# Where the stores of the halves stand, which chunks carry the splitting, and in what order a layer takes its kept chunks

## The chip, the cores and the metric

The kernel runs on one core of one Trainium2 chip. The metric is the device time of one execution in microseconds (us). The core has TensorE (PE, matmul), VectorE (DVE), ScalarE (ACT), GpSimd (POOL) and SyncE (SP, which here only issues transfers), all of which run their own instruction streams and meet at semaphores.

## What is computed

A graph network over 3125 nodes with 64 features and 103125 edges, four blocks one after another, each adding its result to x. Three places matter here:

```python
h = max(layernorm(x), 0)
# block 0: ten hops with the unweighted adjacency (counts)
h0 = h @ W + b
for _ in range(10):
    agg = segment_sum((h * norm_src)[src], dst)
    h = 0.9 * agg * norm_dst + 0.1 * h0
x = x + h
# block 1: three layers with the weighted adjacency (float32 edge weights)
h = max(layernorm(x), 0)
for W, b in (1, 2, 3):
    h = segment_sum((h @ W)[src] * norm[:, None], dst) + b     # ReLU after the first two
x = x + h
# block 2: attention over the edges; before it
h = layernorm(max(layernorm(x), 0)) * g + b ;  q, k, v = h @ Wq, h @ Wk, h @ Wv
```

## The kernel before

Both adjacency matrices are held densely. The unweighted one (`counts`, float16) stays in SBUF. The weighted one was written to HBM by `stage_build` as 196 blocks of 16 destination nodes (`aw`, float32, 128 x 400 each, 200 KB). Nodes are 25 rows of 128 (`NCH`); destinations are computed in 7 chunks (`NDC`): six of 512 columns and a seventh, narrow one of 64.

**Hops, `stage_layer0_hops` (L770).** Ten hops of seven chunks. PE, for each chunk c: the product (25 matmuls of 128x512, L840) into bank c % 4, then `back(t, c - 1)` (L824), eight small matmuls that turn the chunk before it, for which ACT must have copied that chunk from its bank (`copied`, L874). DVE then mixes it into the next hop's operand (`mix`, L961 to L965). The count of mixed chunks, `mixed`, gates the next hop's product.

Beside it the float32 blocks are split for the layers into a high and a low float16 half. For each block i: SP loads it into `ring[i % 4]` (L906), DVE sums its columns (`reduce`, L926, counted by `reduced`), ACT casts the high half (`high`, L867), POOL subtracts to get the low half (L895, `lo_done`). Two blocks fill one of two buffers `split`, and SP stores the pair (400 KB, L908, `halves`). ACT's first cast into a buffer waits for that buffer's store (`stored`); a load into the ring waits for `reduced` and `lo_done` of the block that was there. Each pair of hops handles 40 blocks (the last one 36), four behind each chunk until they are used up: all seven chunks of the even hop, and three of the odd one. ACT's order is: copy of chunk c, its four casts, copy of chunk c + 1. DVE's order is: mix of chunk c, its four reduces. After every eight blocks PE turns a column of sums into degrees (`degrees`, L833).

SP's loop, per four blocks, before:

```python
for k in range(4):
    sp.wait_ge(reduced, g * 4 + (k - 3)); sp.wait_ge(lo_done, g * 4 + (k - 3))
    sp.dma_start(ring[k], ...)              # load of block 4g + k
    if k % 2:
        sp.dma_start(halves[...], flat(k // 2))     # store of a pair of four blocks ago
```

**Layers, `stage_layer1` (L984).** Three layers of seven chunks. A chunk of the weighted matrix is read back as 16 stored pairs (L1018). Chunks 0 to 4 (`STREAM` = 5) are streamed in each layer through two buffers of `m.big`; chunk 5 and the narrow chunk 6 are loaded once and kept. PE's product is 50 matmuls of 128x512 (L1047) and up to four for the self loops (L1052); `back` (L1064) multiplies the chunk before by W. A load into a streamed buffer waits on SP until the product that read it is done (`prod_done`). After a layer DVE takes a maximum, POOL spreads it (L1093), and DVE halves the new operand (`halve`, L1106 and L1107), for which the next layer's first product waits. Order of chunks: 0 to 6. The three W and b (nine transfers) are issued by SP after the first two big loads; PE waits for them (`s_in`) after the first product. ACT's first work in the stage is a sqrt for the norm.

**Attend tables, `stage_attend_tables` (L1211).** Ten small loads, PE transposes Wk, Wv and We once all ten have landed (L1263), DVE copies them (L1324 to L1327) and the product with Wp (L1330), and then runs two norms over 128x1600 (L568 to L576, with L1333 between), two products (L1336, L1337), and `hn` goes to HBM and to PE. POOL clears a region in the beginning (L1258).

## Time and profile before

| what | us |
|---|---|
| median of 3 runs | 4331.68 |
| lowest, highest | 4321.05, 4349.07 |
| the profiled execution, its own time | 4306.86 |
| its span | 4305.1 |
| mean granted TensorE clock | 0.817 of full speed |
| hops, from PE's first product to the next stage | 870.3 to 1366.4 |
| layers | 1366.4 to about 1694 |
| attend tables | about 1695 to 1754 |

The profile is one execution, with start and duration of each instruction and, for each engine's idle time, the instruction or transfer that ended it. Busy times of engines overlap. A granted clock of 1.00 is 2.4 GHz, 0.50 is 1.2 GHz; a mean between them is a stretch with both. SPq rows are SP issuing a transfer, not the transfer itself. Median landing times run from the issue to the data's arrival.

### The profile page before, as it was taken

How to read it: one execution, taken by the hardware profiler on the slowest of the kernel's cores; microseconds unless marked ns; L12 is line 12 of the kernel's file. 1: busy time of each engine (PE TensorE's matmuls, PEld its weight loads, DVE VectorE, ACT ScalarE, POOL GpSimd, SP SyncE). 2: the span in 40 equal slices, each digit the busy share in tenths (PEclk: the TensorE clock that was granted, in tenths of full speed). 3: DMA queues.
4: the chain of work that ended last, by engine and by line, in shares of the span. 5: the costliest groups of instructions: out<-in, count | busy, mean ns of one | idle time of the engine just before them, and what ended most of it. 6: DMA issues, size and time to landing. Idle time of an engine off the chain costs nothing. (4 is left out here: it accounts for less than half of the span.)

```text
span 4305.1 us, 80877 instructions
## 1 busy us (share of the span) xinstructions
PE 3180.1 (74%) x17608; PEld 2011.1 (47%) x17608; DVE 1986.0 (46%) x6727; ACT 1584.7 (37%) x4586; POOL 1621.8 (38%) x1763
## 2 busy tenths in 40 slices
PE   3787877778886686477777777777764777787777
PEld 2444444444443343356656656656652444444445
DVE  5666666555555112344444444444743444444442
ACT  1555555222221000233333333333422444444444
POOL 2000000033332000466666666665005666666660
PEclk6899898989997888687787887777956888888885
DMA  1111111155556974322222222222102222222220
GB/s 32 58 59 58 59 58 60 34 161 153 158 176 228 377 305 185 72 54 54 53 55 55 55 54 53 55 54 54 31 2 60 62 65 65 66 63 65 66 59 9
DMA packets 417246, 370.53 MB, mean 86 GB/s; under 512 B 175145, under 2 KB 341769, under 8 KB 416873
## 3 DMA queue, kind: packets, MB, share of 16 engines
q1 hardware_dynamic: 367512, 316.11, 23.1%
q0 software_dynamic: 46144, 48.98, 6.2%
q8 instruction: 192, 3.15, 0.3%
q14 instruction: 182, 1.48, 0.1%
q10 hardware_dynamic: 3216, 0.82, 0.1%
HBM read 279.70 MB, written 86.00 MB: 85 GB/s over the span
## 5 line engine op out<-in xcount | busy, mean ns | idle before, releaser
L1413 POOL DMA_INDIRECT big<-row_table,src x806 | 762.9, 947 | 542.7 <-issue 185.0
L1731 POOL DMA_INDIRECT big<-message_table,src x610 | 611.3, 1002 | 331.7 <-DVE big L1858 174.1
L1438 PE MATMUL banks<-big 97*128 x902 | 400.3, 534 | 142.2 <-issue 136.3
L1454 PE MATMUL banks<-big 128*128 x1804 | 348.8, 326 | 174.0 <-ACT big L1470 109.8
L486 PE MATMUL banks<-work 128*128 128x226 f16 x1197 | 350.3, 293 | 147.0 <-issue 131.4
L1454 PEld LDWEIGHTS banks<-big 128*128 128x128 f32 x1804 | 313.9, 245 | 200.8 <-issue 200.3
L1769 PE MATMUL banks<-big 128*128 128x512 f16 x1225 | 393.6, 439 | 14.1 <-DVE big L1846 14.1
L840 PE MATMUL banks<-big,work 128*128 128x512 f16 (+1 forms) x1750 | 354.7, 362 | 17.8 <-DVE work L973 17.4
L1503 DVE TENSOR_REDUCE big<-banks 128x1 f32<-128x256 f32 x451 | 189.8, 421 | 334.6 <-PE banks L1438 190.2
L1470 ACT COPY big<-banks 128x256 f32<-128x256 f32 x451 | 170.1, 377 | 453.6 <-remote 201.8
L1778 PE MATMUL banks<-big 128*64 x1804 | 246.7, 267 | 122.2 <-issue 106.8
L1778 PEld LDWEIGHTS banks<-big 128*64 128x64 f32 x1804 | 173.1, 163 | 348.8 <-issue 348.1
L487 PE MATMUL banks<-work 128*128 128x200 f16 x1197 | 335.7, 280 | 0.0
L488 PE MATMUL banks<-work 128*128 128x200 f16 x1197 | 327.1, 273 | 0.0
L895 POOL TENSOR_TENSOR work<-work 128x400 f16<-128x400 f32 x196 | 184.0, 961 | 322.0 <-ACT work L867 322.0
L486 PEld LDWEIGHTS banks<-work 128*128 128x128 f16 x1197 | 121.9, 102 | 373.8 <-issue 360.5
L1520 DVE SCALAR_TENSOR_TENSOR big<-big,banks 128x97 f32 x451 | 142.7, 316 | 325.9 <-remote 193.3
L429 POOL COPY work<-work 128x100 f16<-128x100 f16 x120 | 35.9, 300 | 666.9 <-DVE work L452 649.8
L512 ACT ACTIVATE work<-banks 128x800 f32<-128x800 f32 x196 | 164.5, 839 | 330.0 <-PE banks L488 330.0
L1864 DVE TENSOR_SCALAR big<-big 128x512 f16<-128x512 f16 x1225 | 282.2, 286 | 3.2 <-issue 0.2
L1047 PE MATMUL banks<-big,work 128*128 128x512 f16 x900 | 218.1, 407 | 86.4 <-DMA big<-weights_halves 49.9
L1858 DVE TENSOR_TENSOR big<-banks,big 128x128 f32<-128x128 f32 x305 | 87.4, 287 | 411.9 <-remote 290.0
(320 smaller groups left out, 5863.6 us busy)
## 6 DMA issues: line engine op xcount, KB each, us to landing
big<-weights_halves SPq DMA_DIRECT2D x16, 6400.0 KB, 20.3
weights_dense<-work SPq DMA_DIRECT2D x196, 200.0 KB, 1.9
work<-weights_dense SPq DMA_DIRECT2D x196, 200.0 KB, 3.1
weights_halves<-work SPq DMA_DIRECT2D x98, 400.0 KB, 3.7
big<-q_table SPq DMA_DIRECT2D x451, 64.0 KB
big<-in_ef SPq DMA_DIRECT2D x403, 64.0 KB
big<-in_ea SPq DMA_DIRECT2D x403, 32.0 KB
big<-row_table,src POOLq DMA_INDIRECT x806
```

Of the source, the lines that this page charges most:

```text
L486: pe.matmul(to(CW, CW + CAW), rows[:, 0, t, :], cols[:, t, :], start=False, stop=True, skip_group_check=True)
L487: pe.matmul(to(0, CW), rows[:, 1, t, :], cols[:, t, 0:CW], start=False, stop=True, skip_group_check=True)
L488: pe.matmul(to(0, CW), rows[:, 2, t, :], cols[:, t, 0:CW], start=False, stop=True, skip_group_check=True).then_inc(vis_done, 1)
L840: ins = pe.matmul(m.PB[c % 4][:, 0:width(c)], z[k][:, a, :, :], counts[:, a, c * DC:c * DC + width(c)], start=(a == 0), stop=(a == NCH - 1))
L1047: pe.matmul(out, z[l % 2][:, a, :, :], st[buffer(l, c)][:, 0:n // BP, s, a * BP:(a + 1) * BP], start=(a == 0 and s == 0), stop=False)
L1413: po.indirect_dma_start(rows[:, t % RT, s, 0:D], None, x_t.rearrange("a p c -> (a p) c"), bass.IndirectOffsetOnAxis(ap=m.src2[:, s, t:t + ...
L1438: pe.matmul(psS[v % 2], qT[v % R][0:XW, :], XF[0:XW, bass.ds(slot, 1), :].rearrange("p t e -> p (t e)"), start=False, stop=True).then_inc( ...
L1454: ins = pe.matmul(psA[v % 2], PT[v % 2][:, s * P:(s + 1) * P], rows[:, bass.ds(slot, 1), s, :].rearrange("p t c -> p (t c)"), start=(s == ...
L1731: po.indirect_dma_start(G[n % R][:, s, :], None, g_t.rearrange("a p c -> (a p) c"), bass.IndirectOffsetOnAxis(ap=m.src2[:, s, t:t + 1], ax ...
L1769: pe.matmul(psH[q % 2], table[:, a, :, :].rearrange("p s d -> p (s d)"), hot[n % HOT], start=(a == 0), stop=(a == NCH - 1)).then_inc(hot_u ...
L1778: ins = pe.matmul(psA[v % 4], oh[v % 4][:, s, :], M[:, bass.ds(slot, 1), s, :].rearrange("p t c -> p (t c)"), start=(s == 0), stop=(s == 1))
L1864: dve.tensor_scalar(hot[n % HOT], key[q % 2], float(P * a - CENTER), None, ALU.is_equal).then_inc(hot_ready, 1)
```

## The change

It has five parts.

1. In the hops SP stores a pair as soon as both its blocks are split, ahead of the two loads into their ring places, and without waiting for their `reduced`.
2. Blocks are dealt out as four behind each of chunks 0 to 4 of every hop (`SUMMING` = 5), none behind chunks 5 and 6. `degrees` moves to the steps 4, 6, 9, 11, 13 of a pair's fourteen.
3. In the layers the chunks are taken in the order 0, 1, 5, 2, 3, 6, 4: the kept ones stand between the streamed ones. Chunk 5 is loaded before the narrow one. Counters go by the place in that order.
4. The nine small weights are issued by ACT, ahead of its sqrt.
5. In the attend tables DVE runs the first norm before it waits for the transposes, and the second one before it copies the product with Wp.

```diff
+def blocks_after(k, c, n):
+    at = 4 * (SUMMING * k + c)
+    return range(at, min(n, at + 4)) if c < SUMMING else range(0)
+SUMMING = 5
+DEGREES_AT = (4, 6, 9, 11, 13)
...
-                    if at in (4, 6, 8, 10, 12):
-                        degrees(pair, (at - 4) // 2, isinstance(pair, int) and pair == 0)
+                    if at in DEGREES_AT:
+                        degrees(pair, DEGREES_AT.index(at), isinstance(pair, int) and pair == 0)
...
-                    for i in range(4 * (NDC * k + c), min(summed_in(pair), 4 * (NDC * k + c) + 4)):
+                    for i in blocks_after(k, c, summed_in(pair)):
                         high(pair, i)
...
-                for k in range(4):
-                    sp.wait_ge(reduced, g * 4 + (k - 3))
-                    sp.wait_ge(lo_done, g * 4 + (k - 3))
-                    sp.dma_start(ring[k], aw[bass.ds(g * 4 + k, 1), :, :].rearrange("j p c -> p (j c)")).then_inc(w_landed[k], 16)
-                    if k % 2:
-                        sp.dma_start(halves[bass.ds(g * 2 + (k // 2 - 2), 1), :, :].rearrange("j p c -> p (j c)"),
-                                     flat(k // 2)).then_inc(stored[k // 2], 16)
+                for i in range(2):
+                    sp.wait_ge(lo_done, g * 4 + (2 * i - 2))
+                    sp.dma_start(halves[bass.ds(g * 2 + (i - 2), 1), :, :].rearrange("j p c -> p (j c)"), flat(i)).then_inc(stored[i], 16)
+                    for k in range(2 * i, 2 * i + 2):
+                        sp.wait_ge(reduced, g * 4 + (k - 3))
+                        sp.dma_start(ring[k], aw[bass.ds(g * 4 + k, 1), :, :].rearrange("j p c -> p (j c)")).then_inc(w_landed[k], 16)
...
+        ORDER = (0, 1, STREAM, 2, 3, NDC - 1, 4)
...
             load(0, 0)
             load(0, 1)
-            for i in range(3):
-                for half in range(2):
-                    sp.dma_start(w_sb[i][half * D:(half + 1) * D, :], wts[i]).then_inc(s_in, 16)
-                sp.dma_start(b_sb[i], biases[i].partition_broadcast(P)).then_inc(s_in, 16)
+            load(0, STREAM)
             load(0, NDC - 1)
-            load(0, STREAM)
             for n in range(2, 3 * STREAM):
                 l, c = divmod(n - 2, STREAM)
-                sp.wait_ge(prod_done, l * NDC + c + 1)
+                sp.wait_ge(prod_done, l * NDC + ORDER.index(c) + 1)
                 load(n // STREAM, n % STREAM)
...
-                u = l * NDC + c
+                u = l * NDC + ORDER.index(c)
...
-                for c in range(NDC):
+                for i, c in enumerate(ORDER):
                     product(l, c)
...
-                    if c:
-                        back(l, c - 1)
-                back(l, NDC - 1)
+                    if i:
+                        back(l, ORDER[i - 1])
+                back(l, ORDER[-1])
...
         def _(act):
+            for i in range(3):
+                for half in range(2):
+                    act.dma_start(w_sb[i][half * D:(half + 1) * D, :], wts[i]).then_inc(s_in, 16)
+                act.dma_start(b_sb[i], biases[i].partition_broadcast(P)).then_inc(s_in, 16)
...
+            dve_norm(dve, chain, h, xs, tmp, (mean, var), s_var, s_std, 1)
+            chain(dve.tensor_scalar(h, h, 0.0, None, ALU.max))
             dve.wait_ge(s_wt, 1)
             dve.tensor_copy(u_k[:, 0:D], m.PB[6][:, 0:D])
...
+            dve_norm(dve, chain, hn, h, tmp, (mean, var), s_var, s_std, 2)
+            dve.wait_ge(s_in, 160)
             dve.wait_ge(s_wo, HEADS)
...
-            dve_norm(dve, chain, h, xs, tmp, (mean, var), s_var, s_std, 1)
-            chain(dve.tensor_scalar(h, h, 0.0, None, ALU.max))
-            dve_norm(dve, chain, hn, h, tmp, (mean, var), s_var, s_std, 2)
-            dve.wait_ge(s_in, 160)
```

## Rows read from the trace of the kernel before

**Rows 1.** Stretches (start:end, length; busy and count of engines; PE clock, DMA share, GB/s).

```profile
870.26:1366.37 496.11, 419.24 (x2300) 225.28 (x2300) 282.07 (x537) 125.05 (x266) 184.00 (x196) 0.92 0.54 164
1366.37:1693.02 326.65, 242.70 (x1275) 118.86 (x1275) 61.42 (x145) 11.65 (x23) 1.09 (x3) 0.86 0.81 325
1497.00:1516.00 19.00, 15.89 (x66) 6.88 (x67) 6.50 (x23) 0.59 (x1) 0.35 (x1) 0.82 0.19 62
1377.00:1399.00 22.00, 13.29 (x54) 5.63 (x54) 10.79 (x26) 0.81 (x2) 0.38 (x1) 0.73 1.03 417
```

**Rows 2.** The same view: hops 4, 5 and 9, from first product to next.

```profile
1068.49:1122.27 53.78, 41.16 (x230) 22.53 (x230) 32.68 (x63) 14.45 (x31) 21.41 (x24) 0.91 0.51 152
1122.27:1165.96 43.69, 41.74 (x233) 22.13 (x232) 25.63 (x51) 10.85 (x23) 16.03 (x18) 0.95 0.63 188
1315.35:1363.95 48.60, 45.40 (x232) 23.88 (x231) 18.77 (x35) 9.15 (x19) 12.19 (x14) 0.87 0.44 136
```

**Rows 3.** Waits in the hops: engine, line, for what, total us, times, longest.

```profile
ACT work L867 <- DMA weights_halves<-work: 268.6, 87, 8.3
```

**Rows 4.** Order of time, end of hop 4: start, duration, engine, line, [idle before].

```profile
1110.65 0.95 ACT L867 CAST work<-work 128x400 f16<-128x400 f32 x2 [2.65 <-DMA weights_halves<-work]
1111.26 1.84 POOL L895 TENSOR_TENSOR work<-work 128x400 f16<-128x400 f32 x2 [2.24 <-ACT work L867]
1113.87 0.36 SPq L908 DMA_DIRECT2D weights_halves<-work  x1
...
1115.48 1.97 PE L824 MATMUL banks<-work 128*128 128x64 f32 x8 [5.59 <-ACT work L874]
1117.71 0.95 ACT L867 CAST work<-work 128x400 f16<-128x400 f32 x2 [2.29 <-DMA weights_halves<-work]
1122.27 12.91 PE L840 MATMUL banks<-big,work 128*128 128x512 f16 x50
```

**Rows 5.** Order of time, beginning of hop 4.

```profile
1079.30 1.00 PE L824 MATMUL banks<-work 128*128 128x64 f32 x8
1083.24 1.07 SPq L906 DMA_DIRECT2D work<-weights_dense  x2
1085.53 1.00 PE L824 MATMUL banks<-work 128*128 128x64 f32 x8
```

**Rows 6.** Order of time, layers 0 and 1, PE.

```profile
1404.43 13.48 PE L1047 MATMUL banks<-big,work 128*128 128x512 f16 x50 [6.38 <-DMA work<-in_L_gnn_b]
...
1500.11 13.41 PE L1047 MATMUL banks<-big,work 128*128 128x512 f16 x50 [4.65 <-DVE work L1107]
...
1513.58 10.96 PE L1047 MATMUL banks<-big,work 128*128 128x512 f16 x50
...
1533.27 13.91 PE L1047 MATMUL banks<-big,work 128*128 128x512 f16 x50 [7.61 <-DMA big<-weights_halves]
```

**Rows 7.** The page's DMA issues: out<-in, count, size of each, median us to landing.

```profile
big<-weights_halves SPq DMA_DIRECT2D x16, 6400.0 KB, 20.3
work<-weights_dense SPq DMA_DIRECT2D x196, 200.0 KB, 3.1
weights_halves<-work SPq DMA_DIRECT2D x98, 400.0 KB, 3.7
```

**Rows 8.** DVE's line L963 in the hops: duration in ns, min/median/max.

```profile
L963 DVE CAST work<-work x63: 186/293/999, 884.7 to 1317.0; 128x256 f16<-128x256 f32 x54, 64x64 f16<-64x64 f32 x9
```

**Rows 9.** Order of time, hop 9.

```profile
1332.34 0.42 DVE L956 TENSOR_TENSOR work<-banks,colsN 128x256 f32<-128x256 f32 x1 [9.86 <-DMA work<-in_x]
1344.85 1.97 PE L824 MATMUL banks<-work 128*128 128x64 f32 x8 [3.20 <-ACT work L874]
```

**Rows 10.** Order of time, attend tables.

```profile
1695.18 5.43 POOL L1258 MEMSET big<- 32x6400 f32 x1 [96.79 <-POOLq L987]
1705.38 1.81 DVE L568 TENSOR_REDUCE colsN<-work 128x25 f32<-128x1600 f32 x1
1730.75 0.38 SPq L1247 DMA_DIRECT2D row_table<-work  x1
```

More of the change, by code:

```diff
@@ L965, in mix @@
                         dve.tensor_scalar(zn[0:rows, a, 1, :], tc, LO, None, ALU.mult).then_inc(mixed, 1)
-                    for i in range(4 * (NDC * k + c), 4 * (NDC * k + c) + 4):
-                        if i < summed_in(pair):
-                            reduce(pair, i)
+                    for i in blocks_after(k, c, summed_in(pair)):
+                        reduce(pair, i)
                 if k:
@@ L1043, in product @@
                 for a in range(NCH):
-                    if c == 0 and a % GROUP == 0:
+                    if c == ORDER[0] and a % GROUP == 0:
                         pe.wait_ge(s_z, l * NG + a // GROUP + 1)
@@ L1056, in back @@
             def back(l, c):
-                u = l * NDC + c
+                u = l * NDC + ORDER.index(c)
                 pe.wait_ge(copied, u + 1)
@@ L1067, in _ @@
             for l in range(3):
-                for c in range(NDC):
+                for i, c in enumerate(ORDER):
                     product(l, c)
-                    if l == 0 and c == 0:
+                    if l == 0 and i == 0:
                         pe.wait_ge(s_in, 144)
-                    if c:
-                        back(l, c - 1)
-                back(l, NDC - 1)
+                    if i:
+                        back(l, ORDER[i - 1])
+                back(l, ORDER[-1])
         @block.scalar
         def _(act):
+            for i in range(3):
+                for half in range(2):
+                    act.dma_start(w_sb[i][half * D:(half + 1) * D, :], wts[i]).then_inc(s_in, 16)
+                act.dma_start(b_sb[i], biases[i].partition_broadcast(P)).then_inc(s_in, 16)
             for n in range(2):
@@ L1085, in _ @@
                     act.wait_ge(back_done, u - 1)
-                n = width(u % NDC)
+                n = width(ORDER[u % NDC])
                 nc.scalar.copy(rt[u % 2][:, 0:n], m.PB[u % 3][:, 0:n]).then_inc(copied, 1)
@@ L1127, in _ @@
             for u in range(3 * NDC):
-                l, c = divmod(u, NDC)
+                l, c = u // NDC, ORDER[u % NDC]
                 dve.wait_ge(back_done, u + 1)
@@ L1144, in _ @@
                     dve.tensor_tensor(xs[0:rows, a, :], xs[0:rows, a, :], tc, ALU.add).then_inc(mixed, 1)
-                if l < 2 and c == NDC - 1:
+                if l < 2 and c == ORDER[-1]:
                     dve.wait_ge(mixed, u + 1)
```

## The prediction

> **What bounds the kernel now.** I read the table by stretch first, because the diff touches three adjacent stages only. The hops take 496.1 us with PE busy for 419.2; the three layers take 326.7 us with PE busy for 242.7 while DMA averages 325 GB/s, although it runs at 417 when it is fed and drops to 62 in the 19 us around a layer's turn [rows 1]. So the hops wait on something short and frequent, and the layers stream from HBM with holes in the stream.
>
> Hops: an even hop costs 53.8 us and an odd one 43.7, with equal PE work [rows 2]. ACT spends 268.6 us waiting for stores of halves [rows 3], mostly harmless. The order of time shows where it is not: ACT casts a pair at 1110.65, POOL splits it until 1113.10, the store leaves at 1113.87, and the next cast into that buffer is at 1117.71: 7.06 us for a loop that returns once a chunk, against a PE cadence of 1085.53 - 1079.30 = 6.23 us [rows 4, 5]. ACT therefore falls behind. Its copies, queued behind four casts, come late, most of all at the narrow seventh chunk, where PE waits 5.59 us; then the eight matmuls take 1.97 us, not 1.00, and the next two products 12.91, not 10.96 [rows 4, 5, 6]. In an odd hop chunks 3 to 6 have no casts, so its tail is free.
>
> **Hops, a floor.** The odd hop lasts 43.69 with PE idle for 1.95 [rows 2]; 1.95 more is the cold clock (12.91 - 10.96). About 0.5 of the idle time belongs to the turn of the hops. Without waits a hop is 43.7 - 1.95 - 1.4 = 40.3 us.
>
> **Hops, after.** Each hop has 20 blocks in chunks 0 to 4, none in 5 and 6. SP issues a pair's store as soon as it is split, then the two loads. I walk one hop with back(0) at 0 (1079.30). The first load of chunk 1's blocks still waits for `reduced`: 3.94 [rows 5]. Landing takes 3.1, of a store 3.7 [rows 7]. So chunk 1's first cast is at 7.05, the four casts end at 10.1 (the second store waits behind two loads: issue 5.2, landed 8.8), and copy(2) ends at 10.7; PE needs it at 12.46, so it is in time. The loop now is cast to split done 2.45, store issue 0.25 instead of 0.77 (no loads ahead), landing 3.84: 6.5 us. Chunks 2, 3 and 4 start their casts at 13.5, 20.0, 26.5; copies 3 and 4 end at 17.2 and 23.7, due at 18.7 and 25.1. But copy(5) ends at 26.5 + 3.1 + 0.6 = 30.2, and PE, past a narrow product of 0.7, wants it at 26.7: a wait of 3.5. The tail wait survives, and now every hop has one.
>
> DVE's mix is at risk: a cast there took between 293 and 999 ns [rows 8], the long ones while POOL split. In my walk POOL splits from 7.65 to 11.45 and mix(1) begins at 7.3, so it may be pushed by up to 2.3 us, its reduces and the loads behind them too. Walked again with that, copy(3) is 0.5 late, copy(4) 0.1, copy(5) 4.8: 5.4 of waits. I take 4.4, between the two. A wait of 3.20 was followed by matmuls at half pace [rows 9], so I add the clock: 0.9 on the late matmuls, 2.0 on the next products. A hop: 40.3 + 4.4 + 2.9 = 47.6. Before, the first nine take 1315.35 - 870.26 = 445.1, or 49.45 each; gain 1.85 x 9 = 16.6 (ends: 25 and 8.5).
>
> The Trainium skill's "SBUF — State Buffer" (SBUF: two separate sides) says that a VectorE op in a 2-port mode, or with two SBUF inputs against a GpSimd op that reads SBUF, waits out the whole GpSimd op; the 999 ns agree. By it alone the first nine hops would gain the 8.5.
>
> Last hop: 36 - 20 = 16 blocks end in chunk 3, so no tail wait. Before, 48.6 with DVE waiting 9.86 for x [rows 2, 9], since ACT issued that load between casts; now no cast stands after the last chunks of hop 8, it leaves before back(0) of hop 9 by some 13 us and is hidden. After: 40.3 + 2.0 = 42.3, gain 6.3. The last store leaves at 26.7 and lands at 30.4 by the walk, when DVE ends its last mix: I charge 1 for the end of the stage. Hops together: 16.6 + 6.3 - 1 = 22 (14 to 30).
>
> **Layers.** The bytes stay: 16 loads of 6,400 KB, at 417 GB/s 15.7 us each [rows 1, 7]. What changes is when the two streaming buffers come free. Before, c = 5 and 6 are computed last, so for some 24 us PE frees nothing, and after both prefetches have landed DMA stands still until the next layer's first product is done. Then the third chunk is late: product 1 of layer 1 starts at 1513.58, when product 0 ended, and product 2 at 1533.27, so 19.7 us from free to landed [rows 6].
>
> Walk after, t = 0 at the first load. Landings: chunk 0 17.7, 1 33.4, kept 5 49.1, kept 6 51.1, then 2, 3, 4 at 67.1, 82.8, 99 without a hole, and layer 1's chunk 0 at 114.5. PE is bound by them in layer 0 and ends its chunk 4 at 110.5. A turn stays at 5.9 (copy, back, mix, max, halve; a full chunk is last, but only one mix follows), so product (1,0) runs from 116.4 to 129.7. Landed: (1,1) 130.2, (1,2) 129.7 + 19.5 = 149.2, (1,3) 164.9. PE computes (1,1) until 141.6, kept 5 until 153.5, (1,2) until 165.4, (1,3) until 177.3, 6, then (1,4), landed 184.9, until 197.5. Layer 2 likewise: (2,0) 203.4 to 216.7, (2,1) to 228.6, kept 5 to 240.4, (2,2) to 252.3, (2,3) to 264.2, (2,4) landed 271.9, done 284.5, back 286.4. Each warm product is 10.96 + 0.9 for own and back; cold ones 12 to 13.4 [rows 6]. Before: 326.65. Gain 40 (34 to 46: the 19.5 stands four times in the chain, each perhaps 1 off, and a cold product more or less is 1 to 2).
>
> In layer 0 the small weights stand in SP's queue behind two big loads, and product (0,1) waited 6.38 for the last bias, until 1404.43, t = 38.1 [rows 6], where its chunk was there at 33.4. On ACT's queue they leave at once; the 4.6 us are in the walk. Nine issues at the 0.36 of SP's store [rows 4], or a little more, take ACT 3 to 5 us; its first sqrt is due some 8 us in (three quarters of one of the two norms that share the tables' 25.3 us, below). The Trainium skill's "DMA: Bandwidth & Descriptors" (Issuing engines are not separate DMA queues) says that all queues share the 16 engines and only issue time is saved; that is how it is costed.
>
> **Attend tables.** DVE's chain starts at 1705.38 only because PE's transposes waited for ten loads; it ends at 1730.72, and the stage starts at 1695.2 [rows 10]. Norms first: 1695.2 + 25.3 + 1.0 for the six copies now between = 1721.5, gain 9.2. Against it: POOL's memset lasts until 1700.6 [rows 10] and the norm's second instruction may stand behind it for 3.5: gain 5.7. I take 7. The same page on SBUF names that lock for a 2-port VectorE op; by it the gain is 5.7. No run shown has the two together.
>
> **Sum.** 22 + 40 + 7 = 69 us. The profiled execution took 4306.86 (span 4305.1), 25 below the median of 4331.68, 14 below the fastest run. On the median: 4331.7 - 69 = 4263 (1.6%).
>
> **Rivals.**
> 1. The tail wait shrinks so far that the clock does not fall. With landings 0.6 shorter the first cast is at 6.4 and the loops keep PE's pace of 6.3, so copy(5) ends at 25.3 + 3.7 = 29.0 and PE waits 2.3, about the odd hop's 1.95 of short waits, whose granted clock stayed at 0.95 [rows 2]. A hop is then 40.3 + 2.3 = 42.6: gain 6.85 x 9 + 6.3 - 1 = 67, and 4331.7 - 114 = 4218 in all. For: less is in flight at a time, since the first store leaves early. Against: the collisions with POOL lengthen the loop. Chance 0.14.
> 2. The hops gain nothing: full collisions in every chunk, and only the last hop profits (5), layers 36, tables 5: 4331.7 - 46 = 4286. Chance 0.17.
> 3. Layers gain only 15: small issues on ACT stand behind the big loads as on SP's queue, and the sqrt, DVE's norm and the first product start up to 16 late; or freed buffers refill later. 4331.7 - 22 - 15 - 7 = 4288. Against: ACT's queue is not the one that the big loads fill, and it landed x in mid-traffic within 10 us [rows 9]. Chance 0.07.
> 4. Slower: loads are now queued behind a store of 400 KB that waits for both blocks' split, so the blocks' arrival, not the store, closes the loop. If it closes in 9.0 us, waits are 3.5 + 4 x 2.5 = 13.5 and the clock costs 2.9 + 4 x 1.0, a hop 60.7; nine lose 101 and the total is 4331.7 + 101 - 52 = 4381. It decides from 7.65 us: 3.5 + 2.9 + 4 x 2.15 = 15.0 makes a hop of 55.3, 5.8 x 9 = 52, which is all that the last hop, layers and tables give. Against: by the walk a load leaves 0.9 after the split and lands at 4.0, beside the store's 4.1. Chance 0.04.
>
> **Chances.** My forecast 0.58. Range 4210 to 4300: rivals 1 to 3 in it. The measurement tells about 1% (43 us) from no change. Faster by over 1%: all of the forecast but a corner, rival 1, most of 2, half of 3: 0.84. Within 1%: 0.12. Slower: 0.04.
>
> **What would show it.** Even and odd hops of equal length, 46 to 49 us, with one PE wait for ACT of 3 to 5 us at the seventh chunk and almost none in mid-hop; the store's issue 0.25 after POOL's end; a last hop near 42. Layers of about 286 us, DMA over 370 GB/s, no hole at the turns over 5 us, PE's waits for loads only before (1,4), (2,4) and in layer 0. DVE's reduce of the norm beginning at once after the layers. I am wrong if tail waits vanish, if mid-hop waits for `w_landed` appear, or if ACT's first sqrt is late.

## The result

| kernel | median us | lowest to highest |
|---|---|---|
| before, 4 runs | 4339.62 | 4321.05 to 4349.07 |
| changed, 4 runs | 4271.28 | 4263.59 to 4278.55 |

The ratio is 0.9847, 95% interval 0.9805 to 0.9890: 68 us or 1.5% faster, where 69 us was forecast. The profiled executions alone, 4306.86 and 4278.55, differ by only 28: attention and the nodes stage behind it, which the diff leaves as they were, took 1480 us together in the one and 1511 in the other, and the messages stage another 10 more. Stage by stage, up to where the attention begins, the trace is the better measure. The hops are counted from PE's first product, the layers from SP's first load, tables and attention from DVE's or POOL's first instruction, all to about 0.1 us.

| stage | before | changed | gain | forecast |
|---|---|---|---|---|
| hops | 496.1 | 466.7 | 29.4 | 22 |
| layers | 328.8 | 292.9 | 35.9 | 40 |
| attend tables | 59.6 | 58.3 | 1.3 | 7 |
| attention begins at | 1754.8 | 1685.8 | 69.0 | |

The three gains make 66.7; the hops also began 2.2 earlier in this execution, with which the diff has nothing to do. So the sum is right and its terms are each off. First the changed kernel's stretches (columns as in [rows 1]): hops, layers, 19 us around the first turn of the layers, hops 5 and 4, the last hop.

```profile
868.02:1334.69 466.67, 424.02 (x2300) 232.02 (x2300) 305.85 (x537) 130.60 (x266) 186.71 (x196) 0.91 0.53 174
1334.69:1625.83 291.14, 239.06 (x1275) 117.72 (x1275) 62.10 (x147) 11.64 (x23) 1.09 (x3) 0.89 0.92 364
1449.00:1468.00 19.00, 14.61 (x64) 6.70 (x63) 8.23 (x26) 0.59 (x1) 0.35 (x1) 0.82 1.02 402
1104.99:1152.42 47.43, 43.28 (x232) 23.69 (x231) 31.69 (x56) 13.25 (x27) 18.86 (x20) 0.90 0.52 170
1057.60:1104.99 47.39, 42.68 (x230) 23.38 (x230) 31.89 (x57) 13.25 (x27) 19.12 (x20) 0.90 0.53 173
1291.91:1332.43 40.52, 40.51 (x232) 22.12 (x231) 23.20 (x41) 11.43 (x23) 15.25 (x16) 0.97 0.55 182
```

Against [rows 1, 2]: even and odd hops are equal, at 47.4. In the last one PE waits for nothing. DMA moves 364 GB/s through the layers where it moved 325 (the forecast's sign was over 370), and 402 at the turn where it moved 62: the hole is closed. ACT's wait in the hops is no longer for the stores ([rows 3]), for which it now never waits, but for the ring's loads:

```profile
ACT work L877 <- DMA work<-weights_dense: 198.7, 112, 5.7
```

The walk through a hop, in order of time in hop 5 (back(0) is at 1118.39, so 0 of the forecast's walk):

```profile
1118.39 1.00 PE L834 MATMUL banks<-work 128*128 128x64 f32 x8
1122.33 1.07 SPq L918 DMA_DIRECT2D work<-weights_dense  x2
1124.81 0.53 ACT L877 CAST work<-work 128x400 f16<-128x400 f32 x1 [5.63 <-DMA work<-weights_dense]
...
1131.84 0.53 ACT L877 CAST work<-work 128x400 f16<-128x400 f32 x1 [2.37 <-DMA work<-weights_dense]
...
1132.44 2.03 POOL L905 TENSOR_TENSOR work<-work 128x400 f16<-128x400 f32 x2 [2.08 <-ACT work L877]
1132.55 1.12 DVE L971 TENSOR_TENSOR work<-work 128x256 f32<-128x256 f32 x1
...
1133.70 0.92 DVE L972 CAST work<-work 128x256 f16<-128x256 f32 x1
...
1138.84 0.53 ACT L877 CAST work<-work 128x400 f16<-128x400 f32 x1 [2.48 <-DMA work<-weights_dense]
...
1145.12 0.53 ACT L877 CAST work<-work 128x400 f16<-128x400 f32 x1 [1.61 <-DMA work<-weights_dense]
...
1149.80 1.97 PE L834 MATMUL banks<-work 128*128 128x64 f32 x8 [4.00 <-ACT work L884]
...
1152.42 12.05 PE L850 MATMUL banks<-big,work 128*128 128x512 f16 x50
```

The load leaves at 3.94, as before [rows 5]. The first casts of chunks 1 to 4 are at 6.4, 13.5, 20.5 and 26.7 (walk: 7.05, 13.5, 20.0, 26.5), and PE waits 4.00 at the narrow chunk (4.4). Between two of these casts stand 7.0, 7.0 and 6.3 us, and each of them waits for a load. Over hops 0 to 8 PE's wait at the narrow chunk is 3.7 to 4.8, and PE waits in mid-hop only three times, 0.8 at most.

### The profile page after: what moved, and what is told of

It is laid out like the page before. It is cut to its first block and busy times, and to the rows that moved or that the text cites. A ratio compares the mean times of both kernels' runs of the same rounds, so it can differ in the third digit from the quotient of the medians.

```text
span 4276.8 us, 80686 instructions
## 1 busy us (share of the span) xinstructions
PE 3229.8 (76%) x17608; PEld 2043.7 (48%) x17608; DVE 2012.0 (47%) x6727; ACT 1587.1 (37%) x4586; POOL 1616.9 (38%) x1763
## 5 line engine op out<-in xcount | busy, mean ns | idle before, releaser
L1447 PE MATMUL banks<-big 97*128 x902 | 408.9, 545 | 149.0 <-issue 125.8
L1447 PEld LDWEIGHTS banks<-big 97*128 97x128 f32 x902 | 180.4, 248 | 200.3 <-issue 198.4
L1821 ACT ACTIVATE big<-iotaH,rel 128x64 f32<-128x64 f16 x902 | 259.1, 335 | 17.0 <-DVE big L1839 15.5
```

The costliest lines, as they stand in the source:

```text
L1447: pe.matmul(psS[v % 2], qT[v % R][0:XW, :], XF[0:XW, bass.ds(slot, 1), :].rearrange("p t e -> p (t e)"), start=False, stop=True).then_inc( ...
L1821: ins = nc.scalar.activation(away[v % 2][:, s, :], m.iotaH[:, 0:BD], ACT.Abs, bias=m.rel2[:, s, v:v + 1], scale=-1.0)
```

## The experiments

All twelve runs were made on other chips than the first, where the kernel before takes 3903 to 3910 us instead of 4340. The stages ahead of the attention take the same time on all of them: the changed kernel's attention begins at 1685.8 and 1686.6, and a stage that an experiment leaves as it was agrees with the first chip's within some 5 us. So stages are compared, each from one profile. What the same code gives in the changed kernel is the measure of noise: hops 463.5 to 469.0, layers 291.3 to 293.5, tables 53.6 to 58.3. The difference between the chips lies behind these stages; see the last section.

| run | hops | hops 0 to 8, mean | layers | tables | attention begins at |
|---|---|---|---|---|---|
| before | 496.1 | 49.45 | 328.8 | 59.6 | 1754.8 |
| changed | 466.7 | 47.10 | 292.9 | 58.3 | 1685.8 |
| changed again (e12) | 466.3 | 46.89 | 293.5 | 58.3 | 1686.6 |
| store order only (e1) | 456.6 | 45.92 | 330.8 | 59.6 | 1715.0 |
| dealing only (e2) | 500.8 | 50.35 | 327.7 | 59.6 | 1757.3 |
| layers only (e3) | 493.9 | 49.72 | 294.0 | 64.2 | 1719.9 |
| weights on SP (e4) | 466.0 | 46.94 | 294.2 | 56.4 | 1685.5 |
| tables as before (e5) | 463.5 | 46.72 | 293.1 | 59.7 | 1684.3 |
| dealt 22 and 18 (e6) | 441.8 | 44.22 | 293.4 | 53.6 | 1656.8 |
| weights later (e7) | 469.0 | 47.20 | 290.9 | 58.2 | 1686.4 |
| reduces first (e8) | 398.8 | 39.69 | 292.5 | 58.3 | 1618.2 |
| PE kept busy (e9) | 469.0 | 47.20 | 291.3 | 53.1 | 1681.1 |
| short subtraction (e11) | 445.5 | 44.70 | 293.5 | 58.1 | 1666.7 |
| four edits together (e10) | 398.8 | 39.69 | 292.5 | 50.1 | 1613.2 |

### The change again

No edit: the changed kernel beside the others.

> The changed kernel itself once more, beside the others. All the stages that the diff touches end at 1685.8 us in its first profile; expected within 5 us of that, hops 0 to 8 at 46.5 to 47.5 each, tables 53 to 60. Against the kernel before 60 to 72 us faster, whatever this chip takes for the stages behind.

Measured: 3841.96 us against 3909.76, ratio 0.9817 (0.9801 to 0.9834), 67.8 us. The attention begins at 1686.6, within 1 us of the first profile. A single profile can thus be trusted to a few us for these stages.

### Which part of the change pays in the hops

Part 1 alone, in the kernel before:

```diff
-                for k in range(4):
-                    sp.wait_ge(reduced, ...); sp.wait_ge(lo_done, ...)
-                    sp.dma_start(ring[k], ...)
-                    if k % 2: sp.dma_start(halves[...], flat(k // 2))
+                for i in range(2):
+                    sp.wait_ge(lo_done, g * 4 + (2 * i - 2))
+                    sp.dma_start(halves[...], flat(i))
+                    for k in range(2 * i, 2 * i + 2):
+                        sp.wait_ge(reduced, ...)
+                        sp.dma_start(ring[k], ...)
```

> The kernel before with only SP's loop changed (a pair is stored once split, then its two loads). My theory: the store's place ahead of the loads is what shortens the loop of cast, split, store; mid-hop waits of PE for ACT go, the even hop keeps two tail waits of 3.5 to 4.5 us (copies of chunks 5 and 6 stand behind casts) and lasts about 51, the odd hop 42 to 43; the mean of the first nine is about 47 (before 49.45, changed kernel 47.1), so nearly all of the hops' gain comes from this part. Rival: the even dealing out of blocks is what gains; then the mean stays above 49.

Part 2 alone, in the kernel before:

```diff
-                    for i in range(4 * (NDC * k + c), min(summed_in(pair), 4 * (NDC * k + c) + 4)):
+                    for i in blocks_after(k, c, summed_in(pair)):
```

> The kernel before with only the dealing changed (four blocks behind chunks 0 to 4 of every hop, none behind 5 and 6). My theory: the loop stays at 7.0 us and the first cast of chunk 1 at 8.7, so copy(5) is 6 to 8 us late in every hop: hops 0 to 8 last 49 to 51 each, no better than 49.45; the last hop drops from 48.6 to about 41 because it has no casts behind chunks 4 to 6 and x is loaded earlier. Rival: the dealing by itself brings the hops to about 47.

Store order alone, hops 3 and 4; dealing alone, hop 3 (stretches):

```profile
1009.35:1051.88 42.53, 41.98 (x232) 22.46 (x232) 26.96 (x51) 11.76 (x23) 15.79 (x17) 0.93 0.57 185
1051.88:1100.71 48.83, 40.62 (x229) 22.70 (x230) 35.80 (x63) 15.36 (x31) 22.13 (x24) 0.93 0.53 176
```

```profile
1020.59:1072.14 51.55, 42.44 (x232) 23.01 (x232) 28.68 (x56) 12.53 (x27) 18.98 (x20) 0.93 0.52 160
```

The store order alone brings the stage to 456.6, 39.5 us less than before and 10.1 less than the full change. The even dealing gains nothing alone (4.7 us more, hardly outside the noise) and loses 10.1 on top of the store order. The stretches say why: in an uneven pair one hop of two has no casts near its end and costs 42.5, with no fallen clock behind it; dealt evenly, each of the two has the tail wait and the slow clock, 2 x 47.1 = 94.2 against 48.8 + 42.5 = 91.3. With the store order alone ACT waits in the hops for the ring's loads as well (211.8 us) and no longer for a store: the edit took the store out of the chain, and what is left is bound by the loads. The gain that I saw for the dealing, in the last hop, was a gain of the store order too: that hop to the end of its stage takes 51.1 before, 43.3 with the store order alone, 47.7 with the dealing alone, 42.8 with both.

### Where the tail wait comes from

Fewer blocks near the end of each hop, in the changed kernel:

```diff
-    at = 4 * (SUMMING * k + c)
-    return range(at, min(n, at + 4)) if c < SUMMING else range(0)
+    at = sum(DEALT[:NDC * k + c])
+    return range(at, min(n, at + DEALT[NDC * k + c]))
+DEALT = (4, 4, 4, 4, 2, 2, 2, 4, 4, 4, 4, 2, 0, 0)
```

> The changed kernel with the blocks dealt out as 4, 4, 4, 4, 2, 2, 2 in the even hop and 4, 4, 4, 4, 2, 0, 0 in the odd one. Theory: the tail wait is the distance from chunk 4's last cast to PE's early need of copy(5), since the product between is narrow. With two casts fewer there it falls from 4.1 to 1 to 2 us, PE's clock stays up (no 1.97 us matmuls, next products 10.96), and the hops last 41.5 to 43.5 instead of 47.1. Rival: the wait moves to copy(6) and the clock falls as before; the hops last over 45.5.

In order of time, PE, end of hops 4 and 5:

```profile
1086.14 1.77 PE L834 MATMUL banks<-work 128*128 128x64 f32 x8 [1.12 <-ACT work L884]
1088.68 0.48 PE L834 MATMUL banks<-work 128*64 128x64 f32 x2 [0.45 <-ACT work L884]
1089.09 12.99 PE L850 MATMUL banks<-big,work 128*128 128x512 f16 x50
...
1130.60 1.85 PE L834 MATMUL banks<-work 128*128 128x64 f32 x8 [1.64 <-ACT work L884]
```

The waits fell to 1.1 and 1.6 as expected, and the hops to 44.2 only, between what I had expected and the rival's 45.5. The clock still fell, and the next products took 12.99 instead of 10.96. My claim that it stays up after such a short wait was wrong; here it falls when a wait of 1.1 us stands behind the narrow product. Behind a full product it is otherwise: in the run with the dealing alone PE waited 2.35 us in mid-hop, and its matmuls took 1.10 us, not 1.97.

```profile
1047.72 1.10 PE L831 MATMUL banks<-work 128*128 128x64 f32 x8 [2.35 <-ACT work L881]
```

The rest is a second wait in each hop, in part the one that the rival named: 0.4 to 1.6 us for ACT at the last copy of most even hops, and 0.6 to 1.8 for DVE ahead of `degrees` in the odd ones.

The other end of the chain, DVE's reduces ahead of the mix instead of behind it:

```diff
+                    for i in blocks_after(k, c, summed_in(pair)):
+                        reduce(pair, i)
                     dve.wait_ge(back_done, NDC * t + c + 1)
...
-                    for i in blocks_after(k, c, summed_in(pair)):
-                        reduce(pair, i)
```

> The changed kernel, with DVE's four reduces of a chunk put ahead of the mix of that chunk (they were behind it). My theory: the ring's loads are late because their place is freed by a reduce that stands behind the mix, and the mix stands behind back(c), which PE runs one product later; with the reduces in DVE's idle time ahead of the mix, loads leave right after the split, chunk 1's first cast is some 5 us earlier against PE, copy(5) is ready before PE wants it, the tail wait of 3.7 to 4.8 us and the slow clock behind it go. Hops 0 to 8 last 40.5 to 42.5 each instead of 47.1; total 45 to 60 us faster than the changed kernel. Rival: the loop of load, cast, split, load is itself over 6.3 us, then the tail wait shrinks by less than 2 us and the total by less than 20.

Measured: 3774.69 against 3902.61, ratio 0.9669 (0.9639 to 0.9698), 128 us under the kernel before, and hops of 39.7 in the mean: more than I expected (40.5 to 42.5). Stage and hop 6 (stretches), and hop 6 in order of time:

```profile
868.59:1267.40 398.81, 392.60 (x2300) 217.56 (x2300) 300.32 (x538) 134.95 (x266) 186.41 (x196) 1.00 0.62 204
1107.61:1146.95 39.34, 38.98 (x229) 21.62 (x230) 32.09 (x56) 13.72 (x27) 19.14 (x20) 1.00 0.62 204
```

```profile
1110.96 3.04 DVE L935 TENSOR_REDUCE work<-work 128x16 f32<-128x400 f32 x4 [0.44 <-issue]
...
1116.95 0.86 SPq L918 DMA_DIRECT2D work<-weights_dense  x2
...
1118.41 1.00 PE L834 MATMUL banks<-work 128*128 128x64 f32 x8
...
1119.63 1.02 ACT L877 CAST work<-work 128x400 f16<-128x400 f32 x2 [0.44 <-DMA work<-weights_dense]
```

The reduces run in idle time ahead of back(0), the loads leave 1.5 us before back(0) instead of 3.9 behind it, and the first casts are at 1.2 instead of 6.4. PE is busy for 38.98 of 39.34 us and its granted clock is 1.00 in the stage's mean: 68 us out of the hops with two lines moved. This shows the cause of the tail wait: the loads' place in the ring was freed by a reduce that stood behind the mix. The collisions of DVE with POOL are still there (24 of the 63 subtractions of the mix, L975, take over 600 ns where the median is 426, the longest 1201), and PE no longer waits for them.

### DVE against POOL

POOL's subtraction cut to 32 of 400 elements a partition, in the changed kernel. Most of each low half stays zero (DVE clears the buffers once, ahead of the hops), so the layers compute with less exact weights.

```diff
-                    po.tensor_tensor(part(1), ring[k]..., part(0), ALU.subtract).then_inc(lo_done, 1)
+                    po.tensor_tensor(part(1)[:, 0:2, :], ring[k]...[:, 0:2, :], part(0)[:, 0:2, :], ALU.subtract).then_inc(lo_done, 1)
```

> The changed kernel with POOL's subtraction cut from 400 to 32 elements a partition (most of each low half is left zero, so the layers compute with less exact weights). Theory: DVE's mix is no longer stretched by POOL (its L973-like instructions stay under 0.5 us), the loop of a chunk falls from 7.0 to PE's 6.3, since what closes it is reduce, load, cast, not the store; the tail wait falls from 4.1 by about the two stretches of 0.7 to 1.3 to 2.0 to 3.0 us, and the clock still falls: hops 44.8 to 46.2. Rival: the collisions are harmless and the tail wait stays above 3.7.

Two instructions of DVE's mix in the hops, the subtraction and the cast ahead of it (ns, min/median/max), first in the changed kernel, then here, where the lines are one lower:

```profile
L973 DVE TENSOR_TENSOR work<-work x63: 216/426/1186, 882.7 to 1294.1; 128x256 f32<-128x256 f32 x54, 64x64 f32<-64x64 f32 x9
L972 DVE CAST work<-work x63: 186/294/1075, 882.4 to 1293.9; 128x256 f16<-128x256 f32 x54, 64x64 f16<-64x64 f32 x9
```

```profile
L974 DVE TENSOR_TENSOR work<-work x63: 216/426/517, 884.1 to 1274.4; 128x256 f32<-128x256 f32 x54, 64x64 f32<-64x64 f32 x9
L973 DVE CAST work<-work x63: 185/294/366, 883.8 to 1274.2; 128x256 f16<-128x256 f32 x54, 64x64 f16<-64x64 f32 x9
```

The stretched instructions are gone and the hops are 2.4 us shorter each, 44.7. The tail wait was 3.2 in the mean where it was 4.25 (2.7 to 3.4, once 4.6). This agrees with the collisions as the difference between my two walks (3.5 and 4.8 of wait), but it is not shown apart: shorter splitting also lets the loads' other condition, `lo_done`, come earlier. The rest of the 2.4 is partly the clock, which fell in every hop but later in some: the late matmuls took 1.11 in five of nine hops and 1.97 in four, the next two products 12.6 in the mean instead of 13.1.

### The layers

Part 3 alone, in the kernel before, the small weights still on SP's queue:

```diff
+        ORDER = (0, 1, STREAM, 2, 3, NDC - 1, 4)
-                u = l * NDC + c
+                u = l * NDC + ORDER.index(c)
```

> The kernel before with only the order of chunks in the layers changed (kept chunks between streamed ones, chunk 5 loaded before the narrow one), the small weights still on SP's queue after two big loads. My theory: the holes in the stream of loads at the turns close, and the stage takes 290 to 296 us where it took 326.7; hops and tables as before. Rival: the loads run at the rate of HBM in any order and the stage stays above 315.

Measured: 294.0, a gain of 34.8 of the 35.9. The order of chunks is nearly all of it.

The small weights back on SP in the changed kernel, and then on ACT but behind its two sqrts:

```diff
+            for i in range(3):
+                for half in range(2):
+                    sp.dma_start(w_sb[i][half * D:(half + 1) * D, :], wts[i]).then_inc(s_in, 16)
+                sp.dma_start(b_sb[i], biases[i].partition_broadcast(P)).then_inc(s_in, 16)
             load(0, STREAM)
```

> The changed kernel with the nine small weights back on SP's queue behind the first two big loads. In the trace of the changed kernel product (0,1) began 37.4 us into the layers, hardly before the old 38.1, though nothing waited for the weights any more. Theory: their transfers cost the same engine time on either queue, and every later chunk comes as late; the stage (from DVE's first memset to the tables' memset) lasts 292 to 295 against 292.9, so this part is worth 0 to 2 us. Rival (the prediction's walk): the stage is 4 to 5 us longer.

```diff
             for n in range(2):
                 act.wait_ge(s_var, n + 1)
...
+            for i in range(3):
+                for half in range(2):
+                    act.dma_start(w_sb[i][half * D:(half + 1) * D, :], wts[i]).then_inc(s_in, 16)
+                act.dma_start(b_sb[i], biases[i].partition_broadcast(P)).then_inc(s_in, 16)
```

> The changed kernel with ACT issuing the nine small weights behind its two sqrts instead of ahead of them. With them on ACT at the stage's start the first product began at +20.8 us, with them on SP's queue at +18.6. Theory: nine small transfers at the start delay the first big load by 2.2; issued 12 us later they delay only the second, the first product begins at +18.4 to 18.7, product (0,1) near +37.4 as before, and the stage takes 291 to 293 (292.9): no gain, since all nine transfers still stand before load 2. Rival: the layers' 5 us over my walk come from them, and the stage drops to 288 or less.

First and second product of layer 0, in order of time: changed kernel (the stage starts at 1334.69), weights on SP (1334.9), weights later (1337.3):

```profile
1355.48 12.91 PE L1052 MATMUL banks<-big,work 128*128 128x512 f16 x50 [23.06 <-DMA big<-weights_halves]
...
1372.05 12.64 PE L1052 MATMUL banks<-big,work 128*128 128x512 f16 x50 [3.44 <-DMA big<-weights_halves]
```

```profile
1353.53 12.66 PE L1056 MATMUL banks<-big,work 128*128 128x512 f16 x50 [20.94 <-DMA big<-weights_halves]
...
1373.50 12.91 PE L1056 MATMUL banks<-big,work 128*128 128x512 f16 x50 [7.09 <-DMA work<-in_L_gnn_b]
```

```profile
1356.88 12.46 PE L1052 MATMUL banks<-big,work 128*128 128x512 f16 x50 [21.91 <-DMA big<-weights_halves]
...
1374.26 12.30 PE L1052 MATMUL banks<-big,work 128*128 128x512 f16 x50 [4.70 <-DMA big<-weights_halves]
```

The first product starts at +20.8, +18.6 and +19.6, the second at +37.4, +38.6 and +37.0. From issue to landing, the first two big loads take (the median is the mean of the two), in the changed kernel and with the weights on SP:

```profile
DMA to landing us min/median/max: 20.8/28.8/36.8
DMA to landing us min/median/max: 18.6/26.6/34.6
```

The second is issued 0.4 us into the stage, so chunk 1 is there at 37.2 in the changed kernel, and at 35.0 with the weights on SP, where PE then waits for the last bias until 38.6. In the kernel before it was there at 35.1, and with the weights issued later on ACT at 36.8. So on ACT's queue, early or late, the small weights cost the second big load some 2 us; on SP's, behind it, they make themselves late. As a whole the queue is worth about 1 us (294.2 against 292.9 and 293.5). That issuing them later gains is not shown: 290.9 is hardly under the 291.3 of e9, which has the layers of the changed kernel, and the last run below, with the weights issued later, takes the same 292.5 as the one with the reduces first.

### The attend tables and PE's clock

The tables in their old order, in the changed kernel:

```diff
+            dve.wait_ge(s_wt, 1)
+            dve.tensor_copy(u_k[:, 0:D], m.PB[6][:, 0:D])     # and the other copies
             dve_norm(dve, chain, h, xs, tmp, (mean, var), s_var, s_std, 1)
             chain(dve.tensor_scalar(h, h, 0.0, None, ALU.max))
             dve_norm(dve, chain, hn, h, tmp, (mean, var), s_var, s_std, 2)
```

> The changed kernel with the attend tables in their old order (copies first, then both norms). The stage took 59.6 us before and 58.3 changed, though DVE's chain was 6.0 us shorter; with only the layers changed it took 64.2. Theory: the norms-first order is worth the 6 us, and what took 4.6 away is PE's clock, which after the new order of the layers stays at half for some 17 us of this stage's matmuls (before: 7.5); so this kernel's tables take 64 to 65 us. Rival: the order of the tables is worth 1.3 and the 64.2 was chance; then they take 59 to 60.

Measured: 59.7. The 64.2 that I wanted to explain by the layers' order did not come back. Over all profiles the old order takes 59.6 three times, 59.7 and once 64.2, the new one 53.6, 56.4, 58.1, 58.2 and three times 58.3. The chain of DVE is some 6.0 shorter in each of the latter; what varies is how long PE's clock stays low afterwards: 17 us in those of 58 and in the one of 64.2, 7.6 in the one of 53.6 (e6). Changed kernel, from the stage's start (its lines answer [rows 10]):

```profile
1627.56 5.43 POOL L1267 MEMSET big<- 32x6400 f32 x1 [86.95 <-POOLq L995]
1627.60 1.82 DVE L578 TENSOR_REDUCE colsN<-work 128x25 f32<-128x1600 f32 x1 [0.32 <-PEq L995]
...
1629.46 3.57 DVE L579 TENSOR_SCALAR colsN<-colsN 128x25 f32<-128x25 f32 x1
...
1657.09 0.38 SPq L1256 DMA_DIRECT2D row_table<-work  x1
1657.12 1.91 PE L1284 MATMUL banks<-ident,work 128*64 128x128 f32 x8 [13.58 <-DVE work L1346]
...
1670.37 1.06 PE L1284 MATMUL banks<-ident,work 128*64 128x128 f32 x4
...
1674.31 0.63 PE L1284 MATMUL banks<-ident,work 128*64 128x128 f32 x4
```

PE's four transposes take 1.06 us until 1674.3, 17.2 us after PE set in, and 0.63 only then. In the kernel before that point came 7.5 us after PE set in. So 6.0 gained on DVE and 4.7 given back on PE.

Forty matmuls on PE that nothing reads, ahead of the tables' transposes:

```diff
                 pe.matmul(m.PB[4 + 3 * hd][0:XW, 0:D], u_v[part, :], w_p[part, :], start=True, stop=True).then_inc(s_wo, 1)
+            for _ in range(40):
+                pe.matmul(m.PB[0][:, 0:P], m.ident[:, :], m.ident[:, :], start=True, stop=True)
```

> The changed kernel with forty 128x128 float32 matmuls on PE between its product with Wp and the tables' transposes; nothing reads what they write. They add work and no result. Theory: the tables' matmuls run at half clock only because PE has been idle; with PE busy while DVE norms, its transposes and products run at full clock from the beginning, and the stage takes 49 to 53 us instead of 58.3. Rival: the clock is not what makes them slow, or is not raised by such work; then the stage stays at 58 or, if the added work ends late, longer.

```profile
1643.84 11.84 PE L1280 MATMUL banks<-ident 128*128 128x128 f32 x80
1657.49 1.07 PE L1286 MATMUL banks<-ident,work 128*64 128x128 f32 x8 [1.82 <-DVE work L1348]
...
1660.10 1.06 PE L1286 MATMUL banks<-ident,work 128*64 128x128 f32 x4
...
1663.96 0.63 PE L1286 MATMUL banks<-ident,work 128*64 128x128 f32 x4
```

Measured: 53.1, just outside the expected 49 to 53. The first eight transposes take 1.07 us instead of 1.91, then some 3 us run slow before the clock is up. The clock is what the 5 us were; that the matmuls bring it is shown here and once more below, while e6 had most of it without them.

### All together

Reduces first, later weights and the forty matmuls, and with them one edit that is new here, POOL's memset in five pieces of 1,280 elements:

```diff
-            po.memset(q_all[D + DE:P, :, :], 0.0).then_inc(s_zero, 1)
+            for j in range(0, JN, 10):
+                ins = po.memset(q_all[D + DE:P, j:j + 10, :], 0.0)
+            ins.then_inc(s_zero, 1)
```

> The changed kernel with the reduces ahead of the mix, the small weights behind ACT's sqrts, the tables' memset in five pieces and forty idle matmuls ahead of the tables' transposes. Theory: hops 39.4 each (68 us less in the stage), layers 292, tables 50 to 51 (DVE's second instruction of the norm waits at most 1.2 instead of 3.57: 2.4 less; full clock: 5 less); 74 to 80 us faster than the changed kernel. Rival: the pieces follow one another so closely that DVE still waits until the last; then tables 53 and 72 us.

```profile
1564.95 0.41 DVE L579 TENSOR_SCALAR colsN<-colsN 128x25 f32<-128x25 f32 x1
```

Measured: 3765.62 against 3909.76, ratio 0.9621 (0.9603 to 0.9639), and 76.3 us under the changed kernel's 3841.96 in the same runs. Tables 50.1. DVE's instruction waits 0.2 instead of 3.4 us. This version beats both kernels.

## Why the prediction was right, and where only in sum

**Hops.** The main line stood: the store's way back shortened, PE's mid-hop waits went, the tail wait stayed and moved into every hop, with the clock falling behind it. What closes the loop was wrong. The walk gave it to the store (cast, split, store, landing: 6.5 us); in the trace ACT waits for no store at all and 112 times, 198.7 us, for a load, and the loop takes 7.0 twice and 6.3 once. That is the mechanism of rival 4 at a much lower price, and one of the forecast's own signs of being wrong ("mid-hop waits for `w_landed`") appeared, on ACT; PE hardly saw it. The wait of 4.4 is near the measured one (3.7 to 4.8, mean 4.25) since it was set between two walks, of which the second let the loads be pushed. That it came out so well is in part luck.

Of the other terms, late matmuls were +0.9 (1.97 against 1.00) and next products +2.0 (13.1 in the mean, so +2.1). The mis-sized term is the floor: 40.3 without waits, where reduces first shows 39.34. The odd hop from which it was taken has three `degrees` products in the open where that even one has one, 0.2 us each, and a wait costs more than its idle time: the step with a wait of 1.16 takes 7.56 us (1141.44 to 1149.00), that is 1.33 over the 6.23 of a step without. The floor is 1.0 too high, the terms on top of it are 0.5 too low in sum, so the forecast is 0.5 a hop too slow (47.6 against 47.1), 4.6 of the 7.4 that the hops gained beyond the forecast. The last hop gave 8.1 by PE's products (48.6 to 40.5) where I said 6.3, since its clock came up sooner (12.28 for the first two products), and the end of the stage cost nothing.

What I did not ask is the sign of each part. I priced parts 1 and 2 in one walk and gave the last hop to the dealing; the dealing alone gains nothing, and with the store order it costs 10.1 us. The walk had the means: its tail wait "in every hop" against one in two was written there, and 40.3 + 2.9 + 4.4 twice is more than once that and once 42.3.

The page "SBUF — State Buffer" of the Trainium skill (SBUF: two separate sides) was weighed by 8.5 us for nine hops against 25 without collisions. 21.2 were measured; the collisions are there (up to 1186 ns for 426), but the walk with a collision in every chunk was too dark, and with the reduces first they cost PE nothing.

**Layers.** 35.5 by the forecast's own limits (326.65 to 291.14) for 40. From layer 1's first product the walk holds: 169.0 us to the end (walk 170.0); the turn is 5.8 (5.9); no wait for loads from (1,0) to (1,3). The failed step is the start: t = 33.4 for chunk 1 became 37.4, and with it everything that the loads bind; chunk 4's load, which can start only when product (0,2) is done, adds to it, and layer 1's first product starts at 122.2 where the walk has 116.4. The spacing of the loads for kept 5, 2 and 3 is near the forecast, 15.5 to 15.6 and 2 for the narrow one. The 33.4 was no reading, although the forecast says of the kernel before that its chunk "was there" then: there it landed at 35.1. So 1.7 of the 4 us are in the kernel before as well, and some 2 come with the nine small transfers of 256-byte rows, which the walk put beside the big loads at no cost (35.0 with them on SP's queue, 37.2 on ACT's). The 4.6 us that I gave part 4 for the earlier product (0,1) were about 1.

**Tables.** DVE's chain ended 6.0 sooner, where I took 7 between 5.7 and 9.2. The lock that the Trainium skill states ("SBUF — State Buffer", SBUF: two separate sides), by which it would be 5.7, agrees with the trace: DVE's second instruction, 25 elements, took 3.57 us and ended when POOL's memset did, and 0.41 with the memset in pieces. My 7, between rule and no rule, was the wrong compromise. The step that failed is one that the text does not have: PE's clock behind the chain. I took the rest of the stage as unchanged work, and it took 4.7 longer. So a gain ahead of a cold engine was partly given back.

**Sum.** +7.4 in the hops, -4.1 in the layers (by stage), -5.7 in the tables, +2.2 at the start: the 69 came out because these cancel, which is luck. Of the rivals none came about as a whole. The first one (no clock fall) had the first cast right, at 6.4, but its loop of 6.3 was 7.0, and the clock fell behind a wait of 1.12 us too. Of the fourth one the mechanism came about, at a small price.

## What to carry to other kernels

Where a ring's place is freed by two readers, put the cheap one ahead of anything that waits for the slow engine: here the reduces behind the mix cost 68 us, as much as the whole change gave. Work dealt out evenly over loop passes can be worse than work bunched in every second one, if each pass pays a fixed price (a cold clock) as soon as any is left near its end. Price the parts of a change apart, and for each stage that ends earlier ask what clock the next engine will find.

## What the runs showed of the hardware

- PE's clock: behind the narrow product, waits of 1.12 and 1.64 us were followed by matmuls at 1.77 and 1.85 us instead of 1.00 and products at 12.99 instead of 10.96; with idle times of at most 0.5 us there it was granted in full from 872 us to the end of the stage at 1267. Behind a full product, 2.35 us of waiting left the matmuls at 1.10. In the tables it came up after 7.5 us of work in the kernel before, after 17.2 in the changed one, after 12.9 and 7.6 in two runs with the changed one's tables (e4, e6), with the same work.
- A VectorE tensor_scalar of 25 elements waits for the whole of a GpSimd memset that runs beside it (3.57 us; the same shape on L583 takes 0.18), while the reduce of 1600 elements ahead of it does not (1.82 in both). Between pieces of 1.16 us it gets in.
- Attention and the nodes stage, with the same code, take 1480 to 1511 us on the first chip and 1230 to 1242 on the others; the messages stage takes 1021 and 1031 against 862 to 865. Below, attention and nodes of the kernel before and the changed one on the first chip, and of the changed one on another (stretches): the granted clock is 0.77 and 0.74 against 0.86, and POOL's own work is the same 762 us.

```profile
1754.80:3235.20 1480.40, 1060.81 (x5791) 861.72 (x5791) 658.29 (x3223) 541.94 (x1797) 762.93 (x806) 0.77 0.24 49
```

```profile
1685.80:3196.60 1510.80, 1097.71 (x5791) 890.30 (x5791) 658.32 (x3223) 541.85 (x1797) 762.89 (x806) 0.74 0.23 48
```

```profile
1686.60:2928.90 1242.30, 961.05 (x5791) 774.44 (x5791) 674.03 (x3222) 553.48 (x1797) 761.72 (x806) 0.86 0.28 58
```

The lower clock is not shown to be the cause: of the 268 us between the second row and the third, PE is busy for 137 more and idle for 132 more. Why the chips differ stays open. The nodes stage alone, without an edit in it, takes 117 to 118 us in five profiles (granted clock 0.58) and 127 to 128 in the other nine (0.50 or 0.51), on the first chip and on others. The three with the old order of the layers are all at 118, nine of the eleven with the new one at 128; that the change costs 10 us there is thus possible and not shown. Stages far from the edit can differ by 30 us between two executions, nearly half of what this change gives, and the span of one profile says less than its stages.
